# Routing in four chunks with kept counts, the last dense tile by column halves, transposes late inside the next tile

## The reference

```
x = x + gnn(xn, src, dst, W1, b1, gamma, beta, W2, b2) + mix(xn, Wq, Wk, Wv, proj, Wo, bo)
# gnn ends in relu(agg + b2), agg the second dense product
flat = layernorm(x)
logits = flat @ Wr.T                      # 8 experts
weights, ids = top_k(logits, 2); weights = softmax(weights)
h = einsum('nc,efc->nef', flat, W1); act = h[:256] * silu(h[256:])
x = x + sum over the two experts of weight * (act @ W2[e].T)
```

## Time and profile before

| what | value |
|---|---|
| median of 3 runs | 1527.35 us (1525.8 to 1531.21) |
| the profiled execution, its own time | 1526.58 us |
| its span, first to last instruction | 1524.9 us |
| TensorE busy | 1423.5 us, 93% of the span |
| VectorE busy | 846.3 us, 55% |
| ScalarE busy | 531.2 us, 35% |
| GpSimd busy | 183.0 us, 12% |
| mean granted clock of TensorE | 0.981 of 2.4 GHz |

### The profile page before, as it was taken

One profiled execution on the slowest core, in us unless ns is written; L12 is line 12 of the kernel. 1 busy time (PEld: TensorE's weight loads), 2 busy tenths in 40 slices (PEclk: granted clock), 3 DMA queues, 4 the chain that ended last, 5 costly groups with the idle time before them and its releaser, 6 DMA issues.

```text
span 1524.9 us, 20038 instructions
## 1 busy us (share of the span) xinstructions
PE 1423.5 (93%) x7735; PEld 1307.4 (86%) x7735; DVE 846.3 (55%) x1535; ACT 531.2 (35%) x617; POOL 183.0 (12%) x182
## 2 busy tenths in 40 slices
PE   6999899999999999999999999999999839999996
PEld 5888889889998898899999999999777639888885
DVE  7464677777777777723666323354667534443330
ACT  4333344354344444423112133322111134544441
POOL 0112210110100101000000000000002252222311
PEclk9999999999999999999999999999999859999998
DMA  9765333242331434768343032221654667887863
GB/s 311 233 160 120 64 62 73 37 81 60 59 78 27 94 78 130 277 150 221 85 131 84 15 110 94 81 80 45 189 158 134 161 175 201 206 218 194 189 153 78
DMA packets 97186, 194.33 MB, mean 127 GB/s; under 512 B 31715, under 2 KB 62426, under 8 KB 95373
## 3 DMA queue, kind: packets, MB, share of 16 engines
q1 hardware_dynamic: 76324, 145.83, 32.6%
q0 software_dynamic: 20768, 47.22, 17.1%
HBM read 129.78 MB, written 73.13 MB: 133 GB/s over the span
## 4 chain that ended last, share of the span: by engine, by line
PE 69%; DMA 13%; DVE 8%; ACT 4%; issue 2%; SPq 1%; POOL 1%; POOLq 0%; ACTq 0%; DVEq 0%
PE slot L1728 24%; PE slot L1800 12%; DMA adj_d<-stage 7%; PE slot L1949 7%; PE slot L1876 6%; PE slot L1917 6%; PE kvb L1949 3%; PE kvb L1840 3%; PE slot L1932 2%; DMA adj_d<-eye_dram 2%; PE slot L1684 2%; PE slot L1825 1%; DMA mix_d<-mixn 1%; DVE qp_l L1407 1%; DVE kT L1139 1%
## 5 line engine op out<-in xcount | busy, mean ns | idle before, releaser
L1728 PE MATMUL slot<-big_hi,slab_h 128*128 128x418 f32 x768 | 195.9, 363 | 18.2 <-DVE qp_l L1407 12.0
L1728 PE MATMUL slot<-big_lo,slab_h 128*128 128x418 f32 x768 | 188.9, 354 | 0.0
L1728 PE MATMUL slot<-big_hi,slab_l 128*128 128x418 f32 x768 | 187.8, 352 | 0.0
L1728 PEld LDWEIGHTS slot<-big_hi,slab_h 128*128 128x128 f32 x768 | 138.8, 189 | 26.5 <-DVE qp_l L1407 16.1
L1728 PEld LDWEIGHTS slot<-big_hi,slab_l 128*128 128x128 f32 x768 | 144.8, 189 | 2.3
L1728 PEld LDWEIGHTS slot<-big_lo,slab_h 128*128 128x128 f32 x768 | 144.7, 189 | 2.0
L811 POOL DMA_DIRECT2D adj_d<-stage x80 | 67.1, 839 | 504.4 <-ACT stage L891 367.4
L1800 PE MATMUL slot<-adj,xs_h 125*128 125x418 f32 x480 | 118.2, 354 | 0.8 <-DVE ztmp L1139 0.5
L1800 PE MATMUL slot<-adj,xs_l 125*128 125x418 f32 x480 | 117.4, 353 | 0.0
L1143 DVE TENSOR_SCALAR oh_src<-lane,src_lo 125x125 bf16<-125x125 f16 x320 | 82.9, 259 | 29.2 <-PE kvb L1605 19.3
L1800 PEld LDWEIGHTS slot<-adj,xs_h 125*128 125x128 f32 x480 | 90.4, 189 | 2.2 <-DVE ztmp L1139 0.7
(11 more groups left out here) (292 smaller groups left out, 2916.1 us busy)
## 6 DMA issues: line engine op xcount, KB each, us to landing
slab_raw<-slabs_dram SPq DMA_DIRECT2D x40, 512.0 KB, 3.8
ws_raw<-w_dram SPq DMA_DIRECT2D x36, 512.0 KB
adj_d<-stage POOLq DMA_DIRECT2D x81, 117.2 KB, 3.1
w_raw<-w_dram SPq DMA_DIRECT2D x9, 1024.0 KB
adj_d<-eye_dram POOLq DMA_DIRECT2D x1, 6250.0 KB, 24.2
raw<-adj_d SPq DMA_DIRECT2D x3, 1828.8 KB
dx<-x_dram SPq DMA_DIRECT2D x10, 448.0 KB
xn_d<-dx SPq DMA_DIRECT2D x10, 448.0 KB
```

Of the source, the lines that this page charges most:

```text
L1728: mm = ten.matmul(ps[:, 512 * q:512 * q + CW], w[a][:, kt, :], big[b][:, kt, CW * q:CW * q + CW], start=(kt == 0 and c == 0), stop=(kt == ...
```

## The change

Five edits, all between the second dense product and the experts:

1. The transposes of tile i−1 stand inside tile i, after k-step 5 (6 in tile 1), on every engine ahead of tile i's own work. So dense tiles alternate between the two slots.
2. The chunks are (0,4), (4,7), (7,9), (9,10). The router product of chunk 1 comes after tile 7 (was: after tile 8); its transposes and position products stand inside tile 8. Chunk 2 follows tile 9, then tile 9 alone.
3. The logits of the last chunk are made token by token: 125 tokens stationary, 16 router columns streaming, so no transposes back.
4. `RW` is parted: `RX` holds what needs the exponential. `RW` also adds `sel` over all tiles so far into `counts`, and the position products use that count: one product in place of one per earlier tile.
5. The last dense tile is made by column halves: 24 products for columns 0 to 511, then 24 for the rest. VectorE's step `NA` adds the residual and does the first half while TensorE makes the second.

The core of the diff:

```diff
-CHUNKS = ((0, 4), (4, 7), (7, 10))
+CHUNKS = ((0, 4), (4, 7), (7, 9), (9, 10))
...
+    in_front = {6: [("RT", 0), ("RK", 0)], 7: [("PX", 0), ("RW", 0), ("RX", 0), ("SL", 0)],
+                8: [("RT", 1), ("RK", 1), ("RW", 1), ("RX", 1)], NT - 1: [("NA", NT - 1)]}
     for i in range(NT):
-        if i == 6:
-            o += [("RT", 0), ("RK", 0)]
-        if i == 7:
-            o += [("PX", 0), ("RW", 0), ("SL", 0)]
-        if i == 9:
-            o += [("RT", 1), ("RK", 1)]
-        o.append(("N", i))
+        o += in_front.get(i, [])
         if i:
             o.append(("FT", i - 1))
-        o += [("LN2", i), ("FL", i)]
-        if i == 5:
-            o.append(("R", 0))
         if i == 8:
-            o.append(("R", 1))
-    o += [("PX", 1), ("RW", 1), ("SL", 1), ("FT", NT - 1), ("R", LAST), ("RT", LAST), ("RK", LAST), ("PX", LAST),
-          ("RW", LAST), ("SL", LAST)]
+            o += [("PX", 1), ("SL", 1)]
+        o += [("N", i), ("LN2", i)]
+        if i == NT - 1:
+            o.append(("R", 2))
+        o.append(("FL", i))
+        if i in (5, 7):
+            o.append(("R", (i - 5) // 2))
+    o += [("RT", 2), ("RK", 2), ("RW", 2), ("FT", NT - 1), ("PX", 2), ("RX", 2), ("SL", 2),
+          ("R", LAST), ("RK", LAST), ("RW", LAST), ("PX", LAST), ("RX", LAST), ("SL", LAST)]
...
+INNER |= {("FT", i) for i in range(NT - 1)}
+AMID = {(6, 3): ("RT", 0), (7, 3): ("PX", 0), (8, 1): ("RT", 1), (8, 6): ("PX", 1)}
...
+                elif kind == "NA":
+                    i = k[1]
+                    half = slice(0, 512)
+                    dve.wait_ge(acc_stored[i % 2], LAND * (i // 2))
+                    dve.wait_ge(xm_landed[i % 2], 2 * LAND * (i // 2 + 1))
+                    link(tt(xm[i % 2][:, :], xm[i % 2][:, :], x_t[i % 2][:, :], ALU.add))
+                    dve.wait_ge(dense_half, 1)
+                    link(tt(acc[i % 2][:, half], sums[SLOT[("N", i)]][:T, half], b2b[:, half], ALU.add))
...
+                        if c < LAST:
+                            link(dve.tensor_reduce(count_f, sel[:, 0:EXP * b].rearrange("p (j e) -> p e j", e=EXP),
+                                                   AX.X, ALU.add))
+                            dve.tensor_copy(counts[:, EXP * c + EXP:EXP * c + 2 * EXP], count_f).then_inc(counted, 1)
...
+                if k[1] == LAST:
+                    for kt in range(KD):
+                        for q in range(2):
+                            mm = ten.matmul(ps[:T, 0:2 * EXP], big[q][:, kt, T * a:T * b],
+                                            wr_p[q][:, 2 * EXP * kt:2 * EXP * kt + 2 * EXP],
+                                            start=(kt == 0 and q == 0), stop=(kt == KD - 1 and q == 1))
...
-                    ten.wait_ge(dve_done, DVED[("RK", c - 1)])
-                    for j in range(a):
-                        ten.matmul(to.rearrange("p (j e) -> p j e", e=EXP), before_t[:, T:],
-                                   sel[:, EXP * j:EXP * j + EXP].unsqueeze(1).to_broadcast([T, b - a, EXP]),
-                                   start=(j == 0), stop=False, skip_group_check=True)
...
+                    ten.wait_ge(counted, c)
+                    count = counts[:, EXP * c:EXP * c + EXP]
+                    ten.matmul(to.rearrange("p (j e) -> p j e", e=EXP), before_t[:, T:],
+                               count.unsqueeze(1).to_broadcast([T, b - a, EXP]),
+                               start=True, stop=False, skip_group_check=True)
...
+                    if i == NT - 1:
+                        for q in range(2):
+                            for kt in range(KD):
+                                for c, (a, b) in enumerate(COMBOS):
+                                    mm = ten.matmul(ps[:T, 512 * q:512 * q + 512], big[b][:, kt, T * i:T * i + T],
+                                                    rows_p[kt][a][:, 512 * q:512 * q + 512],
+                                                    start=(kt == 0 and c == 0), stop=(kt == KD - 1 and c == 2))
+                                if q and kt == 2:
+                                    token_transposes(("FT", i - 1))
+                            mm.then_inc((dense_half, psum_full)[q], 1)
+                        continue
...
+                        if i and kt == (6 if i == 1 else 5):
+                            token_transposes(("FT", i - 1))
```

More of the change, by code:

```diff
@@ L521, in build @@
         ln2_var = sem("ln2_var")
+        dense_half = sem("dense_half")
+        counted = sem("counted")
         ln2_std = sem("ln2_std")
@@ L894, in _ @@
                 kind = k[0]
-                if kind not in ACT_KINDS and kind not in ("LNS", "WR", "E", "X", "DG", "DT", "LN2", "RW"):
+                if kind not in ACT_KINDS and kind not in ("LNS", "WR", "E", "X", "DG", "DT", "LN2", "RX"):
                     continue
@@ L1058, in _ @@
                     a, b = CHUNKS[k[1]]
+                    if k[1] == LAST:
+                        copy(lg2[:, 2 * EXP * a:2 * EXP * b], ps[:T, 0:2 * EXP]).then_inc(act_done, 1)
+                        continue
                     if k[1]:
@@ L1242, in _ @@
                 kind = k[0]
-                if kind not in DVE_KINDS and kind not in ("BASE", "AT", "LN", "LNS", "WR", "BASE2", "EO", "XC", "XD", "H", "LN2", "DG"):
+                if kind not in DVE_KINDS and kind not in ("BASE", "AT", "LN", "LNS", "WR", "BASE2", "EO", "XC", "XD", "H", "LN2", "DG", "NA", "RW"):
                     continue
@@ L1436, in _ @@
                     dve.tensor_copy(mixn[f // (KD - 1)][:, :, :], blocks(ps, NT, 128, T)).then_inc(dve_done, 1)
+                elif k == ("N", NT - 1):
+                    i = k[1]
+                    half = slice(512, D)
+                    dve.wait_ge(psum_full, u)
+                    tt(acc[i % 2][:, half], ps[:T, half], b2b[:, half], ALU.add).then_inc(dve_done, 1)
+                    dve.wait_ge(dve_done, DVED[k])
+                    link(dve.scalar_tensor_tensor(out=acc[i % 2][:, half], in0=acc[i % 2][:, half], scalar=0.0,
+                                                  in1=xm[i % 2][:, half], op0=ALU.max, op1=ALU.add))
+                    link(dve.bn_stats(l2st[:, i, 6:12], acc[i % 2][:, half]))
+                    link(dve.bn_aggr(l2mv[:, 2 * i:2 * i + 2], l2st[:, i, :].rearrange("p (q c) -> p q c", c=6)))
+                    ts(nw[:T, 6 * i:6 * i + 1], l2mv[:, 2 * i + 1:2 * i + 2], LN_EPS, ALU.add).then_inc(ln2_var, 1)
                 elif kind == "N":
@@ L1468, in _ @@
                        rstd[:, j:j + 1], ALU.mult).then_inc(dve_done, 1)
-                elif kind in ("RK", "RW", "SL"):
+                elif kind == "NA":
+                    i = k[1]
+                    half = slice(0, 512)
[4 more added lines that the diff above has]
+                    link(tt(acc[i % 2][:, half], sums[SLOT[("N", i)]][:T, half], b2b[:, half], ALU.add))
+                    link(dve.scalar_tensor_tensor(out=acc[i % 2][:, half], in0=acc[i % 2][:, half], scalar=0.0,
+                                                  in1=xm[i % 2][:, half], op0=ALU.max, op1=ALU.add))
+                    dve.bn_stats(l2st[:, i, 0:6], acc[i % 2][:, half])
+                elif kind in ("RK", "RW", "RX", "SL"):
                     c = k[1]
@@ L1607, in group_product, with router_product @@
                 mm.then_inc(e_full, 1)
+            def router_product(k):
+                a, b = CHUNKS[k[1]]
+                free_slot(k)
+                ps = sums[SLOT[k]]
+                first = T * a - (T * (b - a)) % 2
+                ten.wait_ge(dve_done, DVED[("FT", b - 1)])
+                if k[1] == LAST:
+                    for kt in range(KD):
[3 more added lines that the diff above has]
+                                            start=(kt == 0 and q == 0), stop=(kt == KD - 1 and q == 1))
+                    mm.then_inc(psum_full, 1)
+                    return
+                for kt in range(KD):
+                    for q in range(2):
+                        mm = ten.matmul(ps[:, 0:T * b - first], wr_p[q][:, 2 * EXP * kt:2 * EXP * kt + 128],
+                                        big[q][:, kt, first:T * b],
+                                        start=(kt == 0 and q == 0), stop=(kt == KD - 1 and q == 1))
+                mm.then_inc(psum_full, 1)
             def logit_transposes(k):
```

42 lines of the change are left out of this document (20 added, 22 removed).

## The result

The changed kernel takes 1521.16 us (median of 8 executions, 1515.37 to 1524.1), the kernel before 1530.15 us in the same comparison (8 executions, 1525.8 to 1536.07). The ratio is 0.9939, with a 95% interval from 0.9924 to 0.9954: faster by 0.6%, against a forecast of 0.65% and a predicted time of 1517.4. The profiled execution of the changed kernel took 1522.84 us, its span 1521.2.

The account below looks back on a forecast made before the run. TensorE bounds tiles 2 to 9, then waits on the chain through VectorE and GpSimd's scatters to the first expert product. −0.3 − 9.7 + 0.8 = −9.2 us off 1526.6 gives 1517.4; range 1512 to 1524, forecast itself 1514 to 1520.

Parts of the forecast that it names:

- First tiles: Tile 0's transposes inside tile 1 make TensorE wait, and tile 2 waits for the slot: +1.2 us.
- Tiles 2 to 9: Alternating slots remove the wait for VectorE's read ahead of tiles 3, 4, 5, 7 and 8: −3.5 us.
- Moved in: Tile 8's transposes, chunk 1's position products and two new waits fall inside the dense part: +2.0 us.
- Tile 9 normalised: Tail, counted from tile 9's end: normalised tile done at 4.5 us, was 7.1.
- Subtraction: Tail: tile 9's subtraction, behind chunk 2's ranks, weights and count, done at 9.0 us, was 11.4.
- Sixteen products: Tail: tile 9's logit products on TensorE take 3.1 us, from bounds of 1.9 (full clock) and 3.1 (half).
- Rank to positions: Tail: tile 9's rank-to-positions work takes 4.2 us for one tile, was 5.0; positions at 16.7.
- Last issue: Tail: last scatter issued on GpSimd 18.5 us after tile 9's end, was 28.2: −9.7 us.
- Traffic: Last scatter lands in the last two microseconds of the expert weights' DMA: +0.8 us, bounds nothing to 3.4.
- rivals 1 and 3: 1: last scatter, list, gathers queue behind expert weights, 1521 to 1524 us, chance 0.14; 3: dense waits, 1520 to 1522, 0.15.
- rival 3: Dense part: waits at tiles 1, 8 and 9 come to 4 to 6 us instead of 2; 1520 to 1522, chance 0.15.
- The signs that I named: No sums wait before tiles 3 to 8, one in tile 1, two scatters behind last positions, first expert product near 1240.5.

Follow-up runs that it names:

- slow_loop: Changed kernel plus two unused VectorE reductions per tile in tiles 1 to 7; tile 0's additions to first expert product 162.9 us (changed kernel 154.4).
- no_halves: Changed kernel with the last dense tile in the common form, both column halves together; tile 0's additions to first expert product 155.9 us (changed kernel 154.4).
- warm_logits: Changed kernel plus 43 idle TensorE products in pauses before the last tile's logits; tile 0's additions to first expert product 153.4 us (changed kernel 154.4).
- weights_later: Changed kernel with first expert weights issued some 3.4 us later; tile 0's additions to first expert product 157.2 us (changed kernel 154.4).
- warm_experts: Changed kernel plus 132 idle TensorE products behind the last positions; 1517.33 us, ratio 0.9919 to the kernel before.
- warm_all: Changed kernel plus idle products before logits and experts, and the count moved behind each chunk's positions; 1517.16 us, ratio 0.993 to the kernel before.

## Why the prediction was right, point by point

- *First tiles* +1.2: 8.8 us from tile 0's additions to tile 2's start before, 9.9 after: +1.1. Right.
- *Tiles 2 to 9* −3.5: the period is 12.0 in place of 12.8, five times 0.8: −4.0. Right in kind, 0.5 small, since I had 12.1 and 0.7. That VectorE's loop is under that, 11.1 by my count, is shown by slow_loop (11.0).
- *Moved in* +2.0: tile 9's end moved by −1.3, so this is 1.6. The wait at chunk 1's logits (0.2) did not come, the one at tile 8's transposes was 0.36 (0.5).
- *Tile 9 normalised* at 4.5: 4.7. *Subtraction* at 9.0: 9.0. The halves, forecast as 1.9 us, are worth 1.5 net (no_halves).
- *Sixteen products*, 3.1: 3.4, at a clock of 0.50, so the transposes' row at the half clock (0.2 us each) was the nearer one. The Trainium skill's 104 ns for each load ("TensorE: Matmul & The Clock Gate", LDWEIGHTS) agrees with the 109 ns of warm_logits at a clock of 1.00, not with the 210 at 0.50. And the 0.5 us that I gave to a full clock was 1.0. My own figures left less than either: chunk 2's scatters free GpSimd at 16.9, so the last issue could come at 18.4 in place of 18.5. It was 1.0 since the positions came 0.7 later than forecast and GpSimd was free sooner (16.6).
- *Rank to positions*, 4.2: 4.6, of which 0.4 is one instruction, sel, with 0.56 us in place of 0.17 (below).
- *Last issue* at 18.5: 19.2, by these 0.3 and 0.4. −8.9 in place of −9.7.
- *Traffic* +0.8: 0. This is the term that failed, and in two ways. First, its bounds (1.5 to 4.9 us) were not of scatters. The view in the earlier trace rows takes in every transfer of the list tensor: the 1.5 us are the eight loads of the lists, the 4.9 the one transfer that blanks the tensor at 599.8 us. The one scatter that I had a landing of took 2.59. Second, its place in time was wrong. I had the last scatter land in the last two us of the weights' traffic, taking that to start 2.6 us earlier and to last as long. It started 2.3 earlier, counted from tile 9's end, and was shorter: 11 us from its first issue (1213.93 to 1225.0, and the last of it by 1225.8), where it was 13.6 (1210.93 to about 1224.5), with 3.9 MB moved in both, the stores just ahead included. The last scatter was issued at 1226.13, behind it. Five scatters are issued beside the weights in place of eight; whether that is the reason is not shown. weights_later has the order the other way, and the price is 2.8 us.

The sum was −9.2; by the steps it is −1.3 − 8.9 − 0.1 = −10.3, by the measured ratio −9.3 (0.61% of 1530) and by the two medians −9.0. The dense part came out 1.0 better, the tail 0.8 worse, the traffic 0.9 better. The errors partly cancelled, and the path was right; that −9.2 is within 0.2 of what the times show is luck.

The predicted time is 3.8 us under the measured one, and 3.6 of that is the base: I took the sum off the profiled execution's 1526.58, and the kernel before had 1530.15 in the comparison. So 1521.16 lies outside the 1514 to 1520 that I gave to the forecast itself, among the times of rivals 1 and 3, though neither happened: the last scatters landed in 2.9 and 2.6 us, and the dense part gave 1.3 us where rival 3 has it give most of the gain back. The time alone could not have told these apart; the timelines did.

The signs that I named held where they count a wait or a step. They missed where they name a time on the clock: tile 9's end came at 1206.9 (1201.6 ± 1), the last scatter at 1226.1 (1220), the first expert product at 1246.1 (1240.5). All three carry the 6.6 us by which the early part was later; without it they are 1200.4, 1219.6 and 1239.5. I had taken that part as fixed.

## What to carry to other kernels

Read a change of some us in a long program between two marks on either side of the edits; the total carries the wandering of everything ahead. Before a view's minimum and maximum become bounds, look at which instructions it counts. When a chain through a software queue is shortened, count the queue's items behind the last result first (here two scatters in place of six, 5.9 us of 10.3), and ask of each transfer whether it starts before or after the bulk traffic ends. And where parts of a change are tried alone, ask which of them only stands where it does because another made room.

## What was not expected of the hardware

- **A small scatter lands late while bulk traffic runs.** In the changed kernel the six last landed after 6.4, 6.2, 5.2, 4.9, 2.9 and 2.6 us, the last with no traffic left. With the weights later: 6.6, 6.8, 7.2, 7.4, 5.2 and 4.5. The traffic is not all of it: in warm_experts the last two took 2.6 and 4.2, the later one with the traffic already over, and why is not shown. The Trainium skill ("DMA: Bandwidth & Descriptors", "Anatomy of one DMA" and "Latency and other measured facts") puts the fixed cost of a DMA at about 2 us and says that a lighter load of HBM makes it smaller. The trace agrees in direction: 2.6 us without load, and up to 7.4 with it.
- **Some small VectorE instructions end only with the GpSimd scatter beside them.** In five profiles `sel` or `spots` took 0.31 to 0.56 us in place of 0.17, and in warm_logits and warm_all `hot` took 0.46 and 0.45. All of them began 0.59 to 0.84 us into a scatter and ended within 0.04 us of its end (changed kernel: 1221.73 against 1221.76). Where `sel` or `spots` began in the first 0.46 us of a scatter (no_halves, slow_loop, warm_experts, warm_logits, warm_all) it took 0.17. The other way round, scatters of chunks 0 and 1 took up to 2.22 us, in place of 1.18, beside VectorE's two-input instructions over 1024 columns. What they share is not shown.
- **The clock's price.** Idle products kept the clock at 1.00 at the logits and brought it back at the experts, and 0.1 us per small product with it; but only 1.0 us of the possible 1.6 was to be had at the logits and 0.8 of 2.5 at the experts, because another queue was next in line each time.
